# Maxima of two key chunks as one tile plus the relu of a difference, in the first unit and once in each of the next five

## The reference

```python
w = jnp.einsum('bshd,bzhd->bhsz', q, k)
w = w / jnp.sqrt(jnp.float32(DV))
w = jax.nn.softmax(w, axis=-1)
vw = jnp.einsum('bhsz,bzhd->bshd', w, v)
```

## Time and profile before

| | us |
|---|---|
| median of 3 runs | 1036.03 |
| lowest, highest | 1031.02, 1037.11 |
| profiled execution | 1036.88 |
| its span | 1035.1 |
| TensorE busy in the span | 965.8 |
| VectorE busy | 876.2 |
| ScalarE busy | 810.9 |
| GpSimd busy | 220.6 |

### The profile page before, as it was taken

The page is one execution under the profiler, slowest core; times in us unless marked ns, Lnnn a source line. Parts: engine busy times, 40 slices in busy tenths (PEclk is TensorE's granted clock), DMA queues, the critical chain, the costliest instruction groups (busy, mean ns, idle before and its releaser), DMA issues.

```text
span 1035.1 us, 23103 instructions
## 1 busy us (share of the span) xinstructions
PE 965.8 (93%) x9342; PEld 363.7 (35%) x9342; DVE 876.2 (85%) x1123; ACT 810.9 (78%) x1627; POOL 220.6 (21%) x395
## 2 busy tenths in 40 slices
PE   5999999999999999999999799989998999888988
PEld 2542322233333333333333145423333464332324
DVE  7999999999999999999999788853578777889704
ACT  4149999998999988999998588765774577667886
POOL 4233300003121103221203400141032312301112
PEclk9889999999999999999999789987899999999999
DMA  3520400000000000000000263112100441100000
GB/s 102 172 54 3 138 17 17 2 2 2 2 2 2 2 2 2 1 3 2 2 2 2 70 196 94 41 38 56 37 3 1 122 112 43 47 12 2 1 12 11
DMA packets 41387, 37.05 MB, mean 36 GB/s; under 512 B 5085, under 2 KB 39453, under 8 KB 41281
## 3 DMA queue, kind: packets, MB, share of 16 engines
q1 hardware_dynamic: 39024, 30.20, 10.1%
q0 software_dynamic: 1824, 5.25, 1.8%
q10 hardware_dynamic: 432, 0.13, 0.1%
HBM read 21.92 MB, written 13.30 MB: 34 GB/s over the span
## 4 chain that ended last, share of the span: by engine, by line
PE 53%; DVE 30%; issue 7%; ACT 6%; POOL 2%; DMA 1%; another core or an unknown queue 0%; ACTq 0%; DVEq 0%; POOLq 0%; SPq 0%
DVE mx L1377 26%; PE O L1059 20%; PE T L1024 11%; ACT PT L1637 2%; PE S L993 2%; PE T L1138 2%; PE T L1035 2%; PE S L985 1%; ACT PT L1631 1%; PE S L1189 1%; POOL XP L1994 1%; PE S L998 1%; PE T L943 1%; PE O L912 1%; PE T L1145 1%
## 5 line engine op out<-in xcount | busy, mean ns | idle before, releaser
L1377 DVE TENSOR_REDUCE mx<-S 128x2 f32<-128x1024 f32 (+2 forms) x672 | 755.1, 1179 | 56.6 <-PE S L998 21.3
L1637 ACT ACTIVATE PT<-T 128x512 f32<-128x512 f32 (+2 forms) x1280 | 657.8, 585 | 96.3 <-PE T L1024 41.1
L1059 PE MATMUL O<-PT,Va 128*9 128x256 f32 (+1 forms) x4040 | 337.2, 395 | 4.5 <-ACT Os L1671 4.5
L1024 PE MATMUL T<-Qs,Ks 26*128 26x512 f16 x1024 | 242.9, 394 | 11.9 <-ACT PT L1637 6.3
L985 PE MATMUL S<-Ks,Qs 24*128 24x512 f16 x1024 | 202.7, 394 | 8.1 <-DVE mx L1377 6.0
L1024 PEld LDWEIGHTS T<-Qs,Ks 26*128 26x128 f16 x1024 | 68.0, 91 | 232.1 <-issue 136.3
L1059 PEld LDWEIGHTS O<-PT,Va 128*9 128x9 f32 x4040 | 67.6, 88 | 125.4 <-issue 111.0
L1059 PE MATMUL O<-PT,V 128*17 128x256 f32 (+2 forms) x984 | 83.3, 406 | 1.2 <-ACT Os L1671 0.9
L993 PE MATMUL S<-K,Qs 48*128 48x512 f16 (+3 forms) x320 | 60.1, 359 | 11.7 <-DVE mx L1377 9.8
L985 PEld LDWEIGHTS S<-Ks,Qs 24*128 24x128 f16 x1024 | 48.2, 91 | 31.8 <-DVE mx L1377 24.9
L1035 PE MATMUL T<-Qs,K 50*128 50x512 f16 (+3 forms) x256 | 51.0, 356 | 5.3 <-ACT PT L1637 3.9
(11 more groups left out here) (338 smaller groups left out, 892.8 us busy)
## 6 DMA issues: line engine op xcount, KB each, us to landing
Wg<-in_L_ffn_experts SPq DMA_DIRECT2D x28, 192.0 KB, 2.6
Ks<-in_L_ffn_experts SPq DMA_DIRECT2D x20, 192.0 KB, 2.9
Vf<-sorted_x SPq DMA_DIRECT2D x12, 256.0 KB, 4.6
sorted_y<-Vf SPq DMA_DIRECT2D x12, 256.0 KB, 2.3
rows_q<-q SPq DMA_DIRECT2D x7, 256.0 KB, 2.4
sorted_x<-XP POOLq DMA_DIRECT2D x1, 1792.0 KB, 10.7
Qs<-nrow SPq DMA_DIRECT2D x96, 2.0 KB
Qs<-rows_q SPq DMA_DIRECT2D x8, 192.0 KB, 3.7
```

What stands on the lines that cost most here:

```text
L1024: e.matmul(bank, Ks[r0:r0 + 26, quad, keys], Qs[r0:r0 + 26, quad, CH * c:CH * c + CH], start=True, stop=True, tile_position=(r0, 0)).then_ ...
L1059: m = e.matmul(acc[32 * g:32 * g + d1, lo:hi], v, PT[(2 * j + g // 2) % 4][:, p0 + lo:p0 + hi], start=fresh, stop=True, skip_group_check=n ...
L1377: e.tensor_reduce(mx[:, u % 2, h0:h0 + 2, kb], two[:, :, 0:n], AX.X, ALU.max).then_inc(free, 1)
L1637: e.activation(PT[(2 * j + pair) % 4][:, CH * i + lo:CH * i + CH], bank[:, lo:CH], ACT.Exp).then_inc(free, 1)
```

## The change

max(a, b) = a + relu(b - a). For a *folded* pair of tiles (key chunks 2 and 3 of the same queries and heads) the kernel no longer fills a score tile with chunk 3. TensorE puts q k3 - q k2 into a T bank for each of the two heads (two matmuls each, the first with negated queries from `negs`), ScalarE writes the relu of it to SBUF (`relus`, a ring of four), and VectorE's `tensor_tensor_reduce` adds the score tile of chunk 2 to it and takes the maximum of the sum, once for each head. Slot 3 of `mx` has then to be filled by something: the reduction of chunk 1 writes the maxima of its two halves into slots 1 and 3.

All eight pairs of unit 0 are folded (24 tiles instead of 32), and in units 1 to 5 one pair each (31 instead of 32). The queries are negated by ScalarE for unit 0 and by GpSimd for the others. In the start the value projections, `mod` and the `keep_busy` groups are placed anew.

```diff
+FOLDED = {0: [(qt, pair) for qt in range(4) for pair in range(2)], 1: [(2, 1)], 2: [(2, 1)], 3: [(2, 1)], 4: [(2, 1)], 5: [(2, 1)]}
...
-        return [(qt, pair, kb) for qt, kb in pairs for pair in (1, 0)]
+        return [(qt, pair, kb) for qt, kb in pairs for pair in (1, 0) if kb < 3 or (qt, pair) not in FOLDED.get(u, ())]
...
+    def negate(u):
+        if u in FOLDED:
+            P.negated[u] = len(P.negated) + 1
+            P.stage("negate", u)
+
+    def fold(t, i):
+        key = t[1:4] + (i,)
+        if ("fold",) + key in P.turn:
+            return False
+        if i == 0:
+            P.folds[t[1:4]] = len(P.folds)
+        beside("fold", *key)
...
     def emit_s():
...
+        if L == 0 and u > 0 and t[2:] == score_tiles(L, u)[0]:
+            negate(u)
+        if is_folded(t):
+            for i in range(2):
+                fold(t, i)
         between("s", *t)
+        for t2 in tiles[si[0]:si[0] + (4 if u else 2)]:
+            if is_folded(t2) and t2 not in seen:
+                seen.add(t2)
+                for i in range(2):
+                    due.append(lambda t2=t2, i=i: fold(t2, i))
...
     def do_later():
 
+        if due:
+            due.pop(0)()
+            return
...
-        elif i == 18:
+        elif i == 16:
             beside("mod", 1)
-        elif i in (25, 27, 29, 31):
-            values((i - 25) // 2)
-        if 4 <= i < 25:
-            keep_busy(4 if i in (5, 7, 9, 11, 13, 15, 18) else 8)
+        elif i == 19:
+            values(0)
+        if i == 12:
+            negate(0)
+        if i >= 14:
+            while due:
+                due.pop(0)()
+        if 4 <= i < 22:
+            keep_busy(4 if i in (5, 7, 9, 11, 13) else 8 if i < 14 else 2)
     for i in range(7):
...
         emit_s()
+        if i in (0, 1, 6):
+            values(i + 1 if i < 2 else 3)
...
-        keep_busy(3 if i in (3, 4, 5) else 10 if i < 6 else 10)
+        keep_busy(3 if i in (3, 4, 5) else 6 if i in (0, 1, 6) else 10)
...
+        negs = Vf[:, 256:768].bitcast(F16).rearrange("p (k n) -> p k n", k=2)
+        relus = [Vf[:, o:o + 2 * CH].rearrange("p (i n) -> p i n", i=2) for o in (768, 1792, 5632, 6656)]
...
+                elif name == "fold":
+                    u, qt, pair, i = a
+                    c, quad = UNITS[0][u]
+                    bank, full = opened(("fold",) + tuple(a))
+                    rows_in(c, quad, 2)
+                    rows_in(c, quad, 3)
+                    pe.wait_ge(negated, P.negated[u])
+                    r0 = 64 * pair + 32 * i
+                    q0 = CH * c + 128 * qt
+                    e.matmul(bank, negs[r0:r0 + 24, u % 2, 128 * qt:128 * qt + 128], Ks[r0:r0 + 24, quad, 2 * CH:3 * CH], start=True, stop=False,
+                             tile_position=(r0, 0))
+                    e.matmul(bank, Qs[r0:r0 + 24, quad, q0:q0 + 128], Ks[r0:r0 + 24, quad, 3 * CH:4 * CH], start=False, stop=True,
+                             tile_position=(r0, 0)).then_inc(full, 1)
...
+                    if L == 0 and (qt, pair) in FOLDED.get(u, ()) and kb == 2:
+                        r = relus[P.folds[u, qt, pair] % 4]
+                        for i in range(2):
+                            done(("fold", u, qt, pair, i))
+                            m = e.tensor_tensor_reduce(r[:, i, :], two[:, i, :], r[:, i, :], 1.0, -3.0e38, ALU.add, ALU.max, mx[:, u % 2, h0 + i, 2:3])
+                        m.then_inc(free, 1)
+                        continue
+                    if L == 0 and (qt, pair) in FOLDED.get(u, ()) and kb == 1:
+                        e.tensor_reduce(mx[:, u % 2, h0:h0 + 2, 1:4:2], two[:, :, :].rearrange("p h (s n) -> p h s n", s=2), AX.X, ALU.max).then_inc(free, 1)
+                        continue
...
+                    e.activation(relus[n % 4][:, i, :], bank, ACT.Relu).then_inc(free, 1)
...
+                    e.activation(negs[:, 0, :], Qs[:, 0, 0:CH], ACT.Copy, scale=-1.0).then_inc(negated, 1)
```

More of the change, by code:

```diff
@@ L362, in make_plan @@
     out = dict.fromkeys(units, 0)
-    urgent = []
+    urgent, due, seen = [], [], set()
     si = [0]
@@ L379, in may_score, with is_folded @@
         return may_begin(*tiles[si[0]][:2])
+    def is_folded(t):
+        return t[0] == 0 and t[4] == 2 and t[2:4] in FOLDED.get(t[1], ())
+    def negate(u):
[9 more added lines that the diff above has]
+        beside("fold", *key)
     def emit_s():
@@ L1714, in ac_program @@
                     e.activation(bsg, Sb[turn["up", c, bl][0]][:, 0, :], ACT.Tanh, scale=0.5).then_inc(gate_tanh, 1)
+                elif name == "fold":
+                    u, qt, pair, i = a
+                    bank, free = filled(("fold",) + tuple(a))
+                    n = P.folds[u, qt, pair]
+                    if n >= 4:
+                        u0, qt0, pair0 = fold_keys[n - 4]
+                        done(("s", 0, u0, qt0, pair0, 2))
+                    e.activation(relus[n % 4][:, i, :], bank, ACT.Relu).then_inc(free, 1)
+                elif name == "negate" and a[0] == 0:
+                    done(("pick", "q"))
+                    e.activation(negs[:, 0, :], Qs[:, 0, 0:CH], ACT.Copy, scale=-1.0).then_inc(negated, 1)
                 elif name == "gate":
```

24 lines of the change are left out of this document (22 added, 2 removed).

## The result

| | us |
|---|---|
| median before, after (4 executions each) | 1036.03, 1050.14 |
| ratio, 95% interval | 1.0131 [1.0089, 1.0173] |
| lowest and highest after | 1043.10, 1057.51 |
| profiled execution of after, its span | 1044.98, 1043.2 |

The forecast was 1033 in a range of 1026 to 1040. It is wrong in sign and outside the range. On a second chip the ratio came out as 1.0127 [1.0093, 1.016].

A forecast was written before the change was run, and what follows sets the result against it. Units 1 to 4 were taken to go at VectorE's pace, the other two engines close behind. -5.5 + 2.0 + 1.2 - 0.5 = -2.8 on 1036.9 gave 1034.1, the median 0.9 lower: 1033 us, range 1026 to 1040.

The forecast's parts named there:

- The clock: TensorE in the start: a short low-clock spell of 3.4 us, touching two folded tiles, +1.2 us.
- the clock stays low: Rival, chance 0.2: the clock stays low as in the long spell, TensorE paces tiles 17 to 23; 1038 us.
- Unit 0's maxima: VectorE in unit 0: 8 pairs of 512-column operations replace 16 reductions, 1.32 us instead of 2.27 each, -7.6 us.
- What the pairs wait for: Unit 0 from tile 16 to its end, with waits for bank and loads: 15.6 us instead of 21.1, -5.5 us.
- Unit 1's first seven tiles: Start of unit 1: three value projections now lie here, TensorE takes longer than VectorE, +2.0 us given back.
- Units 1 to 5: One folded pair each: -1.14 first step, -1.3 score pairs, +0.9 VectorE, +1.0 ScalarE relus; sum -0.5 us.
- the relus push the exponentials: Rival, chance 0.15: each pair's 1.05 us of ScalarE relus shows in full, +4.2 us more; 1037 to 1038 us.
- The gain of 1.14 us for the first step: Step loop: 24 tiles over 12 steps instead of 25, so the first step takes two tiles, not three; -1.14 us.
- SyncE's queue gets nothing new: SyncE's load and store queue in the start: the change adds nothing to it, no cost counted.
- Half rate: Rival, chance 0.07: 1.14 us for 512 columns, so 13 pairs save nothing on VectorE; 1042 us.
- All of VectorE's work comes off: Rival, chance 0.13: loads and bank in time, 0.61 us per operation, no low spell; -11.0 us, 1025 us.

The follow-up runs named there:

- clock_held: stop_filled_all with 8 keep-busy matmuls instead of none behind tiles 22 and 23, and 10 or 6 in unit 1's first seven tiles; 1036.56 us, ratio to before 0.9962.
- units1to5_only: The changed kernel with only units 1 to 5 folded, one pair each, and the start of before; 1055.74 us, ratio to before 1.0059.
- bias_later: The changed kernel with the bias matmul of the scaled weights at step 8 instead of step 3; 1046.06 us, ratio to before 0.9987.
- rows_apart: The changed kernel with score tiles of units 1 to 5 reordered to stand beside the other pair of heads; 1049.20 us, ratio to before 1.0053.
- units1to5_apart: The changed kernel with unit 0 unfolded, five pairs in units 1 to 5, rows apart and the bias matmul at step 8; 1035.77 us, ratio to before 0.9988.
- unit0_only: The changed kernel with folded pairs in unit 0 alone; 1049.01 us, ratio to before 1.0016.
- before_rows_same_unit1: The kernel before, with the head pairs of unit 1's score tiles swapped, so 23 of 25 stand on the same rows; 1056.82 against 1045.23 us, ratio 0.9999.
- after_again: The changed kernel, an unchanged copy on another chip; 1061.64 us, ratio to before 1.0127.
- before_again: The kernel before, an unchanged copy on another chip; 1044.73 us, ratio to before 0.9948.
- before_bias_later: The kernel before, nothing folded, with the bias matmul at step 8 instead of step 3; 1036.61 us, ratio to before 0.9988.
- stop_filled: The changed kernel with 28 keep-busy matmuls in TensorE's stop in front of the folds of tile 17; 1055.31 us, ratio to before 1.006.
- store_first: The changed kernel with the late key loads issued behind the query store; 1062.42 us, ratio to before 1.0119.
- busy8: The changed kernel with eight instead of two keep-busy matmuls beside tiles 14 to 21; 1064.50 us, ratio to before 1.0135.
- stop_filled_all: stop_filled with the edits of rows_apart and bias_later, `mod` at tile 12 and 4 keep-busy matmuls instead of 2 beside folded tiles; 1041.18 us, ratio to before 1.0014.

## Why the prediction was wrong, point by point

**The step that failed is "The clock", +1.2 us.** It foresaw a fall, named the reason that applies (TensorE stands before 41 us), and priced two lengths, 3.4 and 10.3 us; it took the short one "by the likeness of the stream". The spell was some 20 us long, and a second one of 24 us, in the step loop, had no term at all. clock_held, where the clock stays up, gives the size: closing maximum of unit 0 at 58.51 against 53.16 us (5.4), from there to the first transposed scores 12.3 against 11.4 (0.9), from these to the closing maximum of unit 1 39.0 against 28.2 (10.8). That is 17.1 us, where the sum had 1.2 (two tiles at 1.86 - 1.32 us each would by its own figures be 1.1). clock_held differs in other things too: rows apart, the bias matmul later and so without the stop of 1.5 us, more keep-busy matmuls, `mod` earlier. So 17 is the size of the low clock with its stop, and not a figure to the tenth. Why the first spell was so long stays open. For the second the runs show it: before's short spell came over score tiles beside the other rows, 1.52 us a tile, and the change took that away (1.94). The rival "the clock stays low", 1038 us, had the right mechanism with a third of its price (1.2 + 2.7 + 1.7 = 5.6 us), since it counted the start alone.

**Unit 0's maxima, -7.6 us, bounds 5.2 and 8.4.** Right in kind. A pair takes 1.22 us, not 1.32: operations are 0.61 apart, and the accumulator's read (0.08 us) lies under the next one. By that 8 x 1.05 = 8.4 us, the end of the bounds.
The Trainium skill, "VectorE: DVE Perf Modes", section "Two Vector instructions with no wait between them", which I had set beside this term, counts such an operation as two instructions; the trace does show two records, but the second costs nothing here.

**What the pairs wait for.** Right in place: TensorE waits 1.98 us for ScalarE's read of the bank. Tile 16 began at 41.13 instead of 42.3, since that read came at 39.11. `mod` cost more, 2.34 instead of 1.43 us, at the low clock. From 39.4 us to the end of unit 0 it took 19.1 us instead of the 15.6 of the sum. At the full clock (clock_held) it took 13.8: unit 0 ends 7.4 us earlier than before, where the sum had 5.5.

**Unit 1's first seven tiles, +2.0.** The forecast had the first transposed scores at 64.7; the change had them at 70.84, clock_held at 64.58. That is in part luck: unit 0 ended 1.8 us earlier there than in the forecast, and from its end it took 11.4 us instead of 9.7, with some twenty more keep-busy matmuls at 0.066 us. The kind of the step was right.

**Units 1 to 5, -0.5.** Wrong too, and in sign. The closing maxima of units 1 to 4 are 36.5, 36.7 and 36.1 us apart, against 37.1, 36.6 and 36.5 before, which looks like a gain; but the ends of the second passes say the contrary. Units 1 to 3 take 2.5 us more at the full clock. Three pairs are made in that time, so it is 0.8 for each, where the sum had 0.18 + 0.2. The other traces agree: from the end of unit 0 to that of unit 3 it is 112.7 us in after, units1to5_only and bias_later, 111.9 in rows_apart, units1to5_apart and clock_held, and 110.2 in before and unit0_only, which have no pairs there. So a pair costs 0.6 us with the rows apart, and the order of the tiles another 0.25. Of the rival "the relus push the exponentials", which put the whole of each pair's 1.05 us on top, more than half is there; whether the relus or the four extra matmuls push, no run separates. The gain of 1.14 us for the first step is not seen by itself, and I didn't ask what its third tile did: it set which rows every later tile stands beside.

**What I had not looked at.** SyncE issues the late loads behind the four loads of unit 0's maxima, the first of them 1.9 us later than before and the last 1.7. Its queue in the kernel after (start, us, what), and then in the kernel before:
```profile
64.77 2.46 SPq L2173 DMA_DIRECT2D Qs<-nrow  x4
67.28 0.40 SPq L2165 DMA_DIRECT2D woT<-in_L_attn_Wo  x1
...
75.24 1.21 SPq L2167 DMA_DIRECT2D K<-cst  x2
```
```profile
65.40 0.40 SPq L2070 DMA_DIRECT2D woT<-in_L_attn_Wo  x1
...
73.57 1.21 SPq L2072 DMA_DIRECT2D K<-cst  x2
```
The bias matmul that needs them stands at a fixed step. It was ready in time at 76.26 us before; after, TensorE waited 1.53 us for it. I had written "SyncE's queue gets nothing new", which is true, and not asked what on it comes later.

**The other rivals.** Half rate: refuted (0.61 us). All of VectorE's work comes off, 1025 us: refuted for the change; the nearest to it, clock_held, had a profiled execution of 1031.59 on another chip.

**How far the cause is shown.** The second spell's length: by the seven and three profiles above, and by the two runs that change the rows alone, rows_apart and before_rows_same_unit1 (the latter in its trace and median, not in its ratio). That moving the bias matmul ends it: by bias_later. What else sets it off is open.
The price of the low clock: the 35 executions of before on one chip lie on a line of 0.37 us of time for each us at the low clock (they scatter 1.5 us about it), and on the other chips such a line has 0.35 to 0.41. The executions of after_again have on average 26 us more low time than those of before beside them, which by that chip's line (0.41) is 11 of the 14.4 us between the means. The other 3.4 aren't the clock's by this estimate; I had expected each execution within 3 us of the line. The two other unfolded kernels with before's order of tiles lie within 0.6 us of their chip's line, before_again and before_bias_later; every folded one lies above it, by 0.8 to 7.4 us in the mean, clock_held by 5.2. So the folding costs something of its own, some of it the 2.5 us of units 1 to 3, and even with the clock held it isn't shown to gain.
The first spell: shown is that it falls behind the stop with and without `mod`, and behind `mod` without a stop, and that with the stops filled the clock held in one profiled execution. Open is why some executions, of the kernel before too, are at the low clock from 25.6 us on, and what in the start's stream decides when it comes back.

## What to carry to other kernels

When a change takes a matmul out of an interleaved stream, ask which rows of the array each neighbour uses afterwards: two matmuls that ran side by side can come to stand in series, which costs 0.25 us a unit here at the full clock and 0.42 us on every 1.52 at the low one, and keeps the clock low for longer. Where an earlier stage becomes shorter or a queue later, look at every matmul with a fixed place that waits for a load, and move it behind the load: here that took the ratio from 1.013 to 0.9987, on another chip. When work is taken out of one stream, time the kernel by the stream that was left: the closing maxima ran ahead while the second pass fell behind. And before freeing an engine by giving TensorE more waits, price the low clock from the longest spell that the trace has at that place, not from the most alike.

## What the runs showed of the hardware that was not expected

- Four stops of TensorE in front of the bias matmul, 1.27, 1.35, 1.53 and 1.58 us (stop_filled, units1to5_only, after, store_first), ended with the low clock or just before it; two, of 0.68 and 0.94 us (unit0_only, busy8), did not. In stop_filled_all the clock fell in a stop of 0.84 us, and in after_again at 81.8 us behind a wait of only 0.47, so length alone doesn't decide.
- TensorE busy all the time doesn't bring the clock back soon: 34.00 of 34 us in before_again. Followed by its return were 28 keep-busy matmuls back to back (3.14 us) and, within 3 to 5 us in each of ten profiles, the step loop's stream with the rows apart.
The Trainium skill, "TensorE: Matmul & The Clock Gate", section "What's actually happening", has activity release the throttle; the trace agrees for the 28 matmuls, and shows streams that keep the engine busy and stay throttled.
- The operation on two wide operands, one in PSUM, with a maximum given out, ran at full rate: 512 columns in 0.61 us.
- Executions of one kernel on one chip differ by 73 to 140 us of low clock (before, 35 executions), and by 25 us in time with it.
